# The router gate on four column groups with stationary weights, its result copied and turned by one transpose

## The reference, cut to what matters

```python
var = jnp.mean(x * x, axis=-1, keepdims=True)
xn = rms_w * (x * jax.lax.rsqrt(var + EPS))
gate = xn @ wg_W + wg_b + (genre_embed @ gg_W + gg_b)      # 8 logits for each token
gate_w = jax.nn.softmax(gate, axis=-1)
topk_w, topk_i = jax.lax.top_k(gate_w, TOP_K)              # 2 of 8
```

## Time and profile before

| | |
|---|---|
| median of 3 runs | 1149.29 us (1147.65 to 1151.28) |
| the profiled execution | 1151.16 us |
| its span | 1149.4 us |
| instructions in the span | 23356 |
| mean granted TensorE clock | 0.993 of full speed |

### The profile page before, as it was taken

How to read it: one execution, slowest core, us unless ns; L and a number is a source line. 1 busy time by engine, 2 the same in 40 slices (tenths; PEclk the granted TensorE clock), 3 DMA queues, 4 the chain that set the end, 5 groups by cost and what they waited for, 6 DMA issues and landing times.

```text
span 1149.4 us, 23356 instructions
## 1 busy us (share of the span) xinstructions
PE 1112.2 (97%) x7466; PEld 780.0 (68%) x7520; DVE 759.8 (66%) x2265; ACT 789.9 (69%) x1752; POOL 509.5 (44%) x837
## 2 busy tenths in 40 slices
PE   8899999999999999999899999989999999999988
PEld 4333434445344453444339999979999999999968
DVE  5887786787867878678744443455555555677547
ACT  2478787887878878788596567646666666666645
POOL 7413254756747567575643663552222222232220
PEclk9999999999999999999899999999999999999999
DMA  8663938558475583754747699664566666633536
GB/s 216 191 198 124 278 122 243 163 175 257 136 229 179 170 241 131 233 179 141 262 135 232 196 278 335 194 149 117 156 181 201 194 194 204 206 54 64 166 92 220
DMA packets 101617, 213.66 MB, mean 186 GB/s; under 512 B 10917, under 2 KB 71341, under 8 KB 93046
## 3 DMA queue, kind: packets, MB, share of 16 engines
q1 hardware_dynamic: 86038, 192.42, 52.6%
q0 software_dynamic: 14304, 18.69, 8.8%
q10 hardware_dynamic: 1152, 1.05, 0.4%
HBM read 239.28 MB, written 74.29 MB: 273 GB/s over the span
## 4 chain that ended last, share of the span: by engine, by line
PE 62%; DMA 5%; issue 4%; POOL 4%; DVE 3%; ACT 2%; another core or an unknown queue 0%; POOLq 0%; DVEq 0%; ACTq 0%
PE bank L1104 31%; PE bank L1206 6%; PE bank L1173 6%; PE bank L1187 5%; DMA x<-yout,rows 4%; PE bank L1191 3%; PE bank L1150 2%; PE bank L1159 1%; PE bank L1224 1%; PE bank L1119 1%; PE bank L1264 1%; POOL x L1993 1%; ACT pt L1372 1%; PE bank L1244 1%; DVE junk L1646 1%
## 5 line engine op out<-in xcount | busy, mean ns | idle before, releaser
L1646 DVE CUSTOM_DVE_ANT_0 junk<-bank,mneg 128x512 bf16<-128x512 f32 x512 | 332.3, 684 | 110.6 <-PE bank L1173 107.9
L1372 ACT ACTIVATE pt<-bank 128x512 f32<-128x512 f32 x512 | 294.2, 598 | 64.1 <-PE bank L1187 25.9
L1993 POOL DMA_INDIRECT x<-yout,rows x78 | 123.8, 1587 | 298.6 <-ACT yout L1456 252.1
L1104 PE MATMUL bank<-hid,w 128*128 128x256 f32 x1872 | 243.7, 287 | 4.7 <-DVE hid L1794 4.7
L1104 PEld LDWEIGHTS bank<-hid,w 128*128 128x128 f32 x1872 | 230.4, 191 | 6.7 <-issue 4.8
L1794 DVE TENSOR_TENSOR hid<-full,hid 128x256 fp32r<-128x256 f32 x312 | 134.2, 436 | 140.3 <-ACT full L1451 134.7
L1446 ACT ACTIVATE hid<-bank,biases 128x256 fp32r<-128x256 f32 x312 | 150.5, 482 | 96.1 <-PE bank L1104 88.7
L1451 ACT ACTIVATE full<-bank,biases 128x256 f32<-128x256 f32 x312 | 149.8, 480 | 0.5 <-DVE hid L1794 0.5
L1191 PE MATMUL bank<-mneg,identb 128*128 128x512 bf16 x332 | 127.2, 383 | 0.0
L1206 PE MATMUL bank<-pt,vaug 128*17 128x512 f32 x1024 | 123.3, 599 | 1.8
L1104 PE MATMUL bank<-w,hid 128*128 128x256 f32 x936 | 122.3, 284 | 2.7 <-DVE hid L1794 2.7
(11 more groups left out here) (184 smaller groups left out, 1459.9 us busy)
## 6 DMA issues: line engine op xcount, KB each, us to landing
w<-split_weights SPq DMA_DIRECT2D x80, 1024.0 KB
w<-split_weights SPq DMA_DIRECT2D x40, 2048.0 KB
split_weights<-w_parts SPq DMA_DIRECT2D x64, 512.0 KB
w_parts<-in_W SPq DMA_DIRECT2D x64, 256.0 KB
split_parts<-parts SPq DMA_DIRECT2D x28, 384.0 KB, 2.6
rows<-routed SPq DMA_DIRECT2D x39, 258.0 KB, 4.1
stacks<-split_parts SPq DMA_DIRECT2D x36, 256.0 KB, 6.8
qst<-split_parts SPq DMA_DIRECT2D x24, 256.0 KB, 6.3
```

The source lines that it names most:

```text
L1104: product = T.matmul(ps, w[p], x[q], start=(k == 0 and n == 0), stop=(k == len(weights) - 1 and n == 2))
L1372: A.activation(pt[n % len(pt)][:, :], ps[:, :], ACT.Exp, scale=float(D) ** -0.5).then_inc(exped.sem, 1)
L1646: V.tensor_tensor_reduce(junk[n % 2][:, :], ring_bank(step)[0][:, :], mneg[:, 0, st, :], 1.0, FLOOR, ALU.add, ALU.max, rowmax[gi % 2][:, h ...
L1993: G.indirect_dma_start(x2_dram, bass.IndirectOffsetOnAxis(ap=rows[j % NS][:, tt, E + 1:E + 2].bitcast(U32), axis=0), yout[j % NY][:, tt], ...
```

## The change

`gate` is now computed the other way round: `wg_wide` (the 8 scaled weight columns with zeros up to 32) is stationary, and 128 tokens of `x1T` stream through. The four blocks of tokens write four groups of 32 partitions of one bank, so that the four products of a feature half lie on four column groups of the array. The result, experts on partitions, is copied by ACT to `gateT` (128x128), and a new stage `gate_turn` transposes it with one product against the identity; the condition's product moves there. `logits` reads the 8 columns of each group of 32. In the order, `gate` comes two yields earlier, `gate_copy` one yield behind it, `gate_turn` two yields behind that, and `logits` one behind `gate_turn`: one yield more in all. `prepare` clears `wg_wide` with a memset.

```diff
+GW = 32
@@ chain
     out.append(("root_x1", b))
-    for _ in range(4):
+    for _ in range(2):
         yield
     out.append(("gate", b))
+    yield
+    out.append(("gate_copy", b))
+    yield
+    yield
+    out.append(("gate_turn", b))
     yield
     out.append(("logits", b))
@@ buffers and signals
+    wg_wide = lasting("wg_wide", [P, KT, GW])
+    gateT = lasting("gateT", [P, P])
+    gate_turned = signal("gate_turned", of("gate_turn"))
+    gate_copied = signal("gate_copied", of("gate_copy"))
-    logits_ready = signal("logits_ready", of("gate"))
+    logits_ready = signal("logits_ready", of("gate_turn"))
-    PREPARED = 1 + KT + 3
+    PREPARED = 2 + KT + 3
...
-                "turn_x1": x1T_ready, "gate": logits_ready,
+                "turn_x1": x1T_ready, "gate": gate_copied, "gate_turn": logits_ready,
@@ tensor_program, gate
                 pe.wait_ge(*x1T_ready.at((b, KT - 1)))
                 pe.wait_ge(prepared, PREPARED)
+                for k in range(KT):
+                    for st in range(ST):
+                        product = T.matmul(ps[GW * st:GW * (st + 1), 0:P], wg_wide[:, k], x1T[:, k, st * P:(st + 1) * P],
+                                           start=(k == 0), stop=(k == KT - 1))
+                product.then_inc(gated.sem, 1)
+            elif name == "gate_turn":
+                b, = at
+                ps = take(misc_bank(step))
+                pe.wait_ge(*gate_copied.at((b,)))
+                pe.wait_ge(ident_made, 2)
                 pe.wait_ge(dma_small, 16 * N_SMALL)
                 pe.wait_ge(constants_made, CONSTANTS)
-                for st in range(ST):
-                    for k in range(KT):
-                        T.matmul(ps[:, st * NX:(st + 1) * NX], x1T[:, k, st * P:(st + 1) * P], wg[:, k],
-                                 start=(k == 0), stop=(k == KT - 1))
-                T.matmul(ps[:, ST * NX:(ST + 1) * NX], condR[:, b:b + 1].to_broadcast([C + 2, P]), ggw[:, :],
-                         start=True, stop=True).then_inc(gated.sem, 1)
+                T.transpose(ps[:, 0:P], gateT[:, :], ident[:, :])
+                T.matmul(ps[:, P:P + NX], condR[:, b:b + 1].to_broadcast([C + 2, P]), ggw[:, :],
+                         start=True, stop=True).then_inc(gate_turned.sem, 1)
@@ scalar_program
             elif name == "logits":
                 b, = at
+                ps, _ = misc_bank(("gate_turn", b))
+                act.wait_ge(*gate_turned.at((b,)))
+                if b:
+                    act.wait_ge(*gate_pool.at(("logits", b - 1)))
+                A.activation(logits[:, :, :], ps[:, 0:(ST + 1) * GW].rearrange("p (s x) -> p s x", x=GW)[:, :, 0:NX],
+                             ACT.Copy).then_inc(logits_ready.sem, 1)
+            elif name == "gate_copy":
+                b, = at
                 ps, _ = misc_bank(("gate", b))
                 act.wait_ge(*gated.at((b,)))
                 if b:
-                    act.wait_ge(*gate_pool.at(("logits", b - 1)))
-                A.activation(logits[:, :, :].rearrange("p s x -> p (s x)"), ps[:, 0:(ST + 1) * NX],
-                             ACT.Copy).then_inc(logits_ready.sem, 1)
+                    act.wait_ge(*gate_turned.at((b - 1,)))
+                A.activation(gateT[:, :], ps[:, 0:P], ACT.Copy).then_inc(gate_copied.sem, 1)
@@ vector_program, prepare
                 V.tensor_copy(flts[:, :], ints[:, :]).then_inc(prepared, 1)
+                V.memset(wg_wide[:, :, :], 0.0).then_inc(prepared, 1)
                 dve.wait_ge(dma_small, 16 * N_SMALL)
+                dve.wait_ge(prepared, 2)
                 for k in range(KT):
-                    V.tensor_scalar(wg[:, k], wg[:, k], rmsw[:, k:k + 1], None, ALU.mult).then_inc(prepared, 1)
+                    V.tensor_scalar(wg_wide[:, k, 0:NX], wg[:, k], rmsw[:, k:k + 1], None, ALU.mult).then_inc(prepared, 1)
```

More of the change, by code:

```diff
@@ L747, in _build @@
     N_SMALL, N_COND, N_WO, N_QUAT = 9, 4, 2 * GH, 7
-    PREPARED = 1 + KT + 3
-    misc_stages = ("project", "project_v", "modulation", "maxima_rows", "project_o", "turn_x1", "gate", "place", "gram",
+    PREPARED = 2 + KT + 3
+    misc_stages = ("project", "project_v", "modulation", "maxima_rows", "project_o", "turn_x1", "gate", "gate_turn", "place", "gram",
                    "eliminate", "turn", "mixed", "combined", "turn_x2")
@@ L788, in evicted @@
         return {"project": rests, "project_v": v_ready, "modulation": gains, "maxima_rows": max_rows, "project_o": o_ready,
-                "turn_x1": x1T_ready, "gate": logits_ready, "place": ranks_ready, "mixed": mixed_ready, "turn": rows_split,
+                "turn_x1": x1T_ready, "gate": gate_copied, "gate_turn": logits_ready, "place": ranks_ready, "mixed": mixed_ready, "turn": rows_split,
                 "turn_x2": x2T_whole, "last": summed, "row": max_found, "col": exped}[name].at(at)
```

## The result

| | before | after |
|---|---|---|
| median of 20 runs each | 1148.37 us (1145.09 to 1153.49) | 1151.45 us (1148.16 to 1155.19) |
| ratio after / before | | 1.0027, 95% interval 1.0016 to 1.0038 |
| the profiled execution | 1151.16 us | 1151.55 us |
| its span | 1149.4 us | 1149.8 us |
| mean granted TensorE clock | 0.993 | 0.994 |

The change costs 3.1 us, 0.27%, where 4.9 us less were forecast; 1151.45 lies above the range. The profiled execution of before is 2.8 us above its median and that of after at its own, so the two spans are almost equal; I compare stretches, not ends.

The account below looks back on a forecast made before the run. TensorE's saturated stream was taken as the bound. Gate -7.4, handovers +2.3, start +0.2 and shift 0 sum to -4.9 us, from 1149.3 to 1144.4 us for the median; range 1139.0 to 1150.5.

Parts of the forecast that it names:

- Moved, one slot: Chain of 65 slots for 64, each next chain a slot later: taken as 0 us, bounds -4.4 to +4.4.
- The gate on TensorE: TensorE per gate: -1.70 us, plus 0.45 column groups, 0.22 switch, 0.11 transpose: -0.92 us, over eight gates -7.4 us.
- the way out: TensorE's switch out of four column groups after the gate's products, costed at 0.13 us.
- The way in: TensorE's switch into four column groups ahead of the gate's products, costed at 0.09 us.
- The handovers: TensorE waiting for ACT's copies around the gate: 0.29 us more per gate, eight times, +2.3 us.
- the second handover: gate_turn on TensorE waits for ACT's copy of the gate: taken as 0.29 us, bounds 0 and 0.9 us.
- rival B: At the gate, the second handover is free and some old 0.29 us goes: -7.2 to -9.5, about 1141.0 us; chance 0.16.
- At the start: prepare on DVE gains a memset and a wait, delaying the modulation's product: 0.2 us once, between 0 and 0.4.
- C: At the gate, weight loads don't overlap running products of another column group: 1147.9 us, no change; chance 0.05.
- F: At the gate, the four column groups run one behind the other: +5.0 us, with the start 1154.5 us; chance 0.06.
- D: Among the experts, 4.4 us of TensorE gaps at 751 and 768 us double: 1148.8 us, no change; chance 0.20.
- E: TensorE waits for ACT twice per gate, at gate_turn and its bank's reuse: +7.0, with the start 1156.5 us; chance 0.08.

Follow-up runs that it names:

- the first experiment: The changed kernel with one yield less between root_x1 and gate, so a chain fills exactly 64 slots: 1141.63 us against 1148.93, ratio 0.9938.
- the shifted kernels: The kernel before with four yields more ending the first chain only: 1164.02 us, ratio 1.0120; with POOL's weight conversions four slots later too: 1157.70 us, ratio 1.0093.

## Why the prediction was wrong, by its own steps

**The step that failed** is "Moved, one slot". It saw that the chain goes to 65 slots where it exactly filled 64, and that each next chain starts a slot later. It followed that drift to batch 5's table and into the experts, and in attention passed over it with "POOL and DVE steps of the chain keep their number". Their number is not their place. They are queued among steps tied to the slots (maxima on DVE, conversions on POOL), and the residual met `scale` with nothing to spare. The term was 0 with bounds of 4.4 us either way; it measured 10.4 us, more than the change could gain. The missing rows were there to read: DVE and POOL at the first `scale` of a batch.

**The gate on TensorE** was right. Removed 1.70 us. The 16 records with the way out take 0.58 us, as forecast (0.45 + 0.13). The way in is 0.09 for 0.09, the transpose 0.11 for 0.11. The condition product became 0.09 us cheaper, which wasn't forecast. Per gate -1.01 for -0.92; by batch lengths -1.00.

**The handovers** (+2.3 us) were too dear. ACT's copy takes 0.270 us (0.275 forecast) and is hidden. In the kernel after TensorE waits for it once, 0.2 us, so the second handover costs nothing. With 64 slots the old one costs what it did: weight loads wait for the logits 3.1 us, as in the earlier trace rows, and TensorE loses the same 0.29 us (L1183 starts at 190.36, 0.51 us behind L1201). It stands in both kernels and so leaves the difference alone; in the drifting kernel it happens to be nearly gone, 0.6 us of such waits. So rival B, 1141.0 us, described the gate, and the first experiment's ratio would put the given median at 1142.2 us.

**At the start** the 0.2 us was about right. The modulation's product starts 0.75 us behind the row ahead of it, and in the kernel before 0.48 (66.75 to 67.23): 0.27 us.

```profile
66.20 0.38 PE L1226 MATMUL bank<-identb,m 128*128 128x128 bf16 x4
66.95 1.02 PE L1177 MATMUL bank<-xw,condS 65*8 65x512 f32 x2 [0.36 <-issue]
```

**Rivals.** C and F fall: the loads and products run side by side. D, the late shift, fails too: TensorE's gaps there didn't double but add up to 2.58 + 2.06 + 0.91 = 5.55 us, against 4.4 in the earlier trace rows and one more of 0.50. From the start of the last `row` product to the end of the span it is 573.5 us before and 573.2 after. Two gates in that stretch save 2 us, so the shift can have cost some 1.7 us there, by one execution of each.

```profile
737.23 7.23 PE L1114 MATMUL bank<-hid,w 128*128 128x256 f32 x48 [2.58 <-DVE hid L1820]
770.12 0.46 PE L1129 MATMUL bank<-elim,ident 128*128 128x128 f32 x2 [2.06 <-DVE elim L875]
780.99 1.66 PE L1114 MATMUL bank<-hid,w 128*128 128x256 f32 x12 [0.91 <-DVE hid L1820]
```

E had the right sign and, in part, the right thought (the drifting slot), but the wrong place: it waited for ACT at the gate, and the wait is DVE's for POOL, a third of a batch away. The text did name what would show it wrong, "TensorE's idle time in attention grows by more than 7 us": TensorE was busy for 530.2 of the 540 us from 60 to 600 before and for 518.3 after, so it went from 9.8 to 21.7, by 11.9 us.

**Not settled:** what holds back the rest of the shifted kernels once the wait for the landing is taken away (DVE's wait for `gt` and the lower granted clock are candidates, and no run takes either away); and whether the residual on another engine would end the sensitivity, which wasn't tried.

## What to carry to other kernels

In an order written out by hand, count the period before adding a slot: a step inserted in a chain that exactly fills it shifts everything that is not part of the chain, so take the slot from a place with room. Before a step is called free to move, look at where each in-order engine meets another with no idle time at all; a view of waits does not list a margin of zero, only the two ends side by side do. And when a change that removes work doesn't pay, move its schedule effect into the old kernel alone: one line there told cause from gain.

## What the runs showed of the hardware that was not expected

**Loads of 32 columns overlap in different column groups.** Each takes 0.109 us, and 16 of them would be 1.74 us one behind the other. They keep the queue busy for 0.38 us in a gate (3.0 us in eight), within the 0.58 us of the products themselves. The Trainium skill (TensorE: Matmul & The Clock Gate, Part 3) has loads overlap running matmuls only when the row group differs; here all groups share their rows, and the measurement decides: they overlap.

**A small DVE step can take almost three times as long beside POOL.** The `scale` at 306.16 us took 1.35 us, while the median of this step before is 0.48. In batches 1 to 4 the first `scale`, right behind the residual, takes that long in both kernels, and a POOL step of 128x512 with two inputs runs beside it:

```profile
306.07 1.16 POOL L1877 TENSOR_TENSOR parts<-rest,parts 128x512 bf16<-128x512 f32 x1
```

With 64 slots and `scale` two slots later the first `scale` of this batch took 0.89 us, beside a shorter POOL step. The Trainium skill (GPSIMD Engine Reference, Specifications) says that the two engines share interfaces and that a DVE instruction with two inputs in memory contends there; the traces agree.
